# Loading and preparing the first row of the second part inside the attention's last pass

## The reference

```
x = x + attention(layernorm(x), Wq, Wk, Wv, Wo)        # 32 heads of 32, 8 key/value heads, rope, causal, softmax
x = x + autocorrelation(layernorm(x), ctx, ctx)        # spectra of q, k, v per channel; corr = ifft(qf * conj(kf)).real
                                                       # top 9 of the sums of corr, softmax, weighted shifted values
x = x + streams(layernorm(x), W_res, W_pre, W_post, ..., gate, W_branch)
        # 24 logits a token; a 4x4 matrix made doubly stochastic by 50 log-space iterations; y = (sum of streams) @ W_branch
```

## Time and profile before

| | us |
|---|---|
| median of 3 runs | 1199.89 |
| the profiled execution | 1201.8 |
| its span | 1200.0 |
| PE busy | 1027.2 |
| DVE busy | 907.2 |
| ACT busy | 600.5 |
| POOL busy | 447.7 |

### The profile page before, as it was taken

How to read it: one execution, slowest core, us unless ns; L and a number is a source line. 1 busy time by engine, 2 the same in 40 slices (tenths; PEclk the granted TensorE clock), 3 DMA queues, 4 the chain that set the end, 5 groups by cost and what they waited for, 6 DMA issues and landing times. The chain is left out here.

```text
span 1200.0 us, 23293 instructions
## 1 busy us (share of the span) xinstructions
PE 1027.2 (86%) x7874; PEld 761.2 (63%) x7874; DVE 907.2 (76%) x2830; ACT 600.5 (50%) x1787; POOL 447.7 (37%) x665
## 2 busy tenths in 40 slices
PE   5889999999999999999863899999999899833328
PEld 4667777877777777778643677777555565422215
DVE  6756886667876667866541787789999999899993
ACT  6624555445555445554433677776546555421215
POOL 0713433234433334333323466665334334203011
PEclk9989999999999999999967999999999999955759
DMA  9111011110111110111014214223222221119407
GB/s 378 39 43 51 28 60 59 59 42 22 54 59 59 50 50 18 59 60 43 25 36 151 79 53 132 93 75 113 95 75 92 76 75 54 48 29 333 130 6 188
DMA packets 47234, 95.71 MB, mean 80 GB/s; under 512 B 5952, under 2 KB 30400, under 8 KB 47168
## 3 DMA queue, kind: packets, MB, share of 16 engines
q1 hardware_dynamic: 47168, 94.91, 23.6%
HBM read 64.48 MB, written 27.26 MB: 76 GB/s over the span
## 5 line engine op out<-in xcount | busy, mean ns | idle before, releaser
L628 POOL TENSOR_TENSOR prob_G<-prob_G,rl 128x512 f32<-128x512 f32 x96 | 99.7, 1040 | 251.0 <-DVE rl L513 251.0
L390 ACT ACTIVATE prob_G<-prob_G,negm 128x128 f32<-128x128 f32 x384 | 149.4, 390 | 82.9 <-DVE negm L455 82.9
L245 PE MATMUL ps_qkv<-w_hi,xT_hi 128*128 128x512 f32 x384 | 156.1, 406 | 17.4 <-DVE prob_G L518 9.3
L246 PE MATMUL ps_qkv<-w_lo,xT_hi 128*128 128x512 f32 x384 | 151.0, 393 | 0.0
L247 PE MATMUL ps_qkv<-w_hi,xT_lo 128*128 128x512 f32 x384 | 150.7, 392 | 0.0
L319 PE MATMUL ps_qkv<-wo_hi,aT_hi 128*128 128x512 f32 x256 | 109.1, 426 | 0.0
L321 PE MATMUL ps_qkv<-wo_hi,aT_lo 128*128 128x512 f32 x256 | 103.1, 403 | 0.0
L320 PE MATMUL ps_qkv<-wo_lo,aT_hi 128*128 128x512 f32 x256 | 103.0, 402 | 0.0
L245 PEld LDWEIGHTS ps_qkv<-w_hi,xT_hi 128*128 128x128 f32 x384 | 72.6, 189 | 43.6 <-issue 20.6
L451 DVE TENSOR_TENSOR prob_G<-ps_s,mask 128x512 f32<-128x512 f32 x96 | 64.9, 676 | 43.9 <-PE ps_s L228 43.3
L480 DVE TENSOR_TENSOR xT_lo<-ps_t,xT_hi 128x512 fp32r<-128x512 f32 x16 | 11.1, 691 | 101.2 <-ACT xT_hi L418 101.2
(11 more groups left out here) (287 smaller groups left out, 2682.6 us busy)
## 6 DMA issues: line engine op xcount, KB each, us to landing
xin<-in_x SPq DMA_DIRECT2D x16, 512.0 KB, 3.3
xres<-in_x SPq DMA_DIRECT2D x16, 512.0 KB, 5.3
x<-xres SPq DMA_DIRECT2D x16, 512.0 KB, 2.6
c_xin<-x SPq DMA_DIRECT2D x16, 512.0 KB, 4.1
c_b_xres<-x SPq DMA_DIRECT2D x16, 512.0 KB, 3.3
rows_x<-c_row SPq DMA_DIRECT2D x64, 128.0 KB, 2.3
m_xm<-rows_x SPq DMA_DIRECT2D x16, 512.0 KB, 8.8
out<-m_ot SPq DMA_DIRECT2D x64, 128.0 KB, 2.3
```

Of the source, the lines that this page charges most:

```text
L245: nc.tensor.matmul(ps_qkv[:, n, :], xT_hi[:, k, :], w_hi[:, k, cols], start=k == 0, stop=False)
L246: nc.tensor.matmul(ps_qkv[:, n, :], xT_hi[:, k, :], w_lo[:, k, cols], start=False, stop=False)
L390: r = nc.scalar.activation(prob(g)[:, j, :], prob(g)[:, j, :], ACT.Exp, bias=negm[:, h:h + 1], accum_out=lsum[:, h:h + 1])
L628: nc.gpsimd.tensor_tensor(prob(g), prob(g), rl[:, g * GROUP:(g + 1) * GROUP].rearrange("p (j o) -> p j o", o=1).to_broadcast([P, GROUP, T] ...
```

## The change

Row 0's buffers of the second part and its constants no longer lie in tensors that are allocated with the second part. A new class `FirstRow` places them at addresses that the attention's projection weights `w_hi` and `w_lo` hold, and keeps them through the second and third part. In the attention's last pass, SP waits until the last projection has read these weights (`qkv_ps` at 3 * B) and issues the eight loads there, between the load of the last residual and the store of the last row. ACT, DVE and POOL do the split of the matrices and of row 0 and its normalisation at the end of what they have in that pass, DVE ahead of the residual. PE's order is the same. Eight tensors of the third part (`m_xm0` to `m_xm7`) are placed by the new class too, and nothing else of the third part changes.

```diff
+class FirstRow:
+    def __init__(self, nc, kept):
...
+        with ExitStack() as shared:
+            self.place(shared, "c_")
+        with ExitStack() as shared:
+            self.mixed = [shared.enter_context(nc.sbuf_tensor(f"m_xm{n}", [P, NS, C], F32)) for n in range(MIXED_IN_FIRST)]
...
                     sp.dma_start(xres[:], x[b]).then_inc(xres_in, 16)
+                    if not project:
+                        sp.wait_ge(qkv_ps, 3 * B)
+                        sp.dma_start(row0.xin[:], x1[0]).then_inc(row0.x_in, 16)
+                        sp.dma_start(row0.mats[:, 0:FWD_W, :], dft[:, 0:FWD_W, :]).then_inc(row0.fwd_in, 16)
+                        sp.dma_start(row0.cin[:], ctx_in[0]).then_inc(row0.cin_in, 16)
+                        sp.dma_start(row0.mats[:, FWD_W:N_DFT, :], dft[:, FWD_W:N_DFT, :]).then_inc(row0.const_in, 16)
+                        sp.dma_start(row0.idf[:], ident).then_inc(row0.const_in, 16)
+                        sp.dma_start(row0.w24_sb[:], w24).then_inc(row0.const_in, 16)
+                        sp.dma_start(row0.base_sb[:], base).then_inc(row0.const_in, 16)
+                        sp.dma_start(row0.wb_sb[:], wb.rearrange("(k p) n -> p k n", k=2)).then_inc(row0.const_in, 16)
...
                     attend_out(1)
+                    if not project:
+                        act.wait_ge(row0.fwd_in, 16)
+                        nc.scalar.activation(row0.fwd_hi[:, :, :], row0.mats[:, 0:4, :], ACT.Copy).then_inc(row0.fwd_hi_done, 1)
+                        act.wait_ge(row0.cin_in, 16)
+                        nc.scalar.activation(row0.c_hi0[:], row0.cin[:], ACT.Copy).then_inc(row0.chi_done, 1)
+                        act.wait_ge(row0.x_in, 16)
+                        act.wait_ge(x1_nb_done, 1)
+                        nc.scalar.activation(row0.xn[:], row0.xin[:], ACT.Identity, bias=norm2[:, 0, 1:2],
+                                             scale=norm2[:, 0, 0:1]).then_inc(row0.xn_done, 1)
+                        act.wait_ge(row0.xn_done, 1)
+                        nc.scalar.activation(row0.xn_hi[:], row0.xn[:], ACT.Copy).then_inc(row0.xnh_done, 1)
...
                     attend_out(1)
+                    if not project:
+                        dve.wait_ge(row0.fwd_hi_done, 1)
+                        nc.vector.tensor_tensor(row0.fwd_lo[:, :, :], row0.mats[:, 0:4, :], row0.fwd_hi[:, :, :].bitcast(F32),
+                                                ALU.subtract).then_inc(row0.fwd_lo_done, 1)
...
                     x1_scale(b - 1)
+                if not project and attend:
+                    pool.wait_ge(row0.chi_done, 1)
+                    TT(row0.c_lo0[:], row0.cin[:], row0.c_hi0[:].bitcast(F32), ALU.subtract).then_inc(row0.clo_done, 1)
+                    pool.wait_ge(row0.xnh_done, 1)
+                    TT(row0.xn_lo[:], row0.xn[:], row0.xn_hi[:].bitcast(F32), ALU.subtract).then_inc(row0.xnl_done, 1)
```

More of the change, by code:

```diff
@@ L44, with sem, place, sb @@
 AX = mybir.AxisListType
-def attention_phase(nc, x, wqkv, wo, ident, causal, rope, x1, norm2):
+MIXED_IN_FIRST = 8
+class FirstRow:
+    def __init__(self, nc, kept):
+        self.nc = nc
+        def sem(name):
+            return kept.enter_context(nc.semaphore("c_" + name))
+        self.const_in, self.fwd_in, self.x_in, self.cin_in = sem("const_in"), sem("fwd_in"), sem("x_in"), sem("cin_in")
+        self.fwd_hi_done, self.fwd_lo_done = sem("fwd_hi_done"), sem("fwd_lo_done")
+        self.xn_done, self.xnh_done, self.xnl_done = sem("xn_done"), sem("xnh_done"), sem("xnl_done")
+        self.chi_done, self.clo_done = sem("chi_done"), sem("clo_done")
+        with ExitStack() as shared:
+            self.place(shared, "c_")
+        with ExitStack() as shared:
+            self.mixed = [shared.enter_context(nc.sbuf_tensor(f"m_xm{n}", [P, NS, C], F32)) for n in range(MIXED_IN_FIRST)]
+    def place(self, stack, prefix):
+        def sb(name, shape, dt=F32, on=stack):
+            return on.enter_context(self.nc.sbuf_tensor(prefix + name, shape, dt))
+        with ExitStack() as shared:
+            whole = sb("c_whole0", [P, D], F32, shared)
+        lo = sb("c_lo0", [P, D], F32R)
+        tensors = (whole, lo, sb("c_hi0", [P, D], F32R), sb("b_idf", [P, P]), sb("mats", [P, N_DFT, P]), sb("fwd_hi", [P, 4, P], F32R),
+                   sb("fwd_lo", [P, 4, P], F32R), sb("w24_sb", [P, KD, NLOG]), sb("base_sb", [P, NLOG]), sb("wb_sb", [P, 2, C]),
+                   sb("xin", [P, D]), sb("xn", [P, D]), sb("xn_hi", [P, D], F32R), sb("xn_lo", [P, D], F32R), sb("cin", [P, D]))
+        if prefix == "c_":
+            (self.c_whole0, self.c_lo0, self.c_hi0, self.idf, self.mats, self.fwd_hi, self.fwd_lo, self.w24_sb, self.base_sb, self.wb_sb,
+             self.xin, self.xn, self.xn_hi, self.xn_lo, self.cin) = tensors
+def attention_phase(nc, x, wqkv, wo, ident, causal, rope, x1, norm2, row0, ctx_in, dft, w24, base, wb):
     with ExitStack() as ctx:
@@ L777, in weave, with autocorrelation_phase @@
             advance(dve, chain, to, 1)
-def autocorrelation_phase(nc, x1, ctx_in, ident, dft, w24, base, wb, norm2, facts, chains, rows_x, rows_y):
+def autocorrelation_phase(nc, x1, ctx_in, row0, norm2, facts, chains, rows_x, rows_y):
     with ExitStack() as ctx:
@@ L793, in sem @@
             return ctx.enter_context(nc.semaphore("c_" + name))
[L795 to L805, removed]
-        xres = sb("b_xres", [P, D])
[L807 to L814, removed]
+        idf, mats, fwd_hi, fwd_lo, w24_sb, base_sb, wb_sb = (row0.idf, row0.mats, row0.fwd_hi, row0.fwd_lo, row0.w24_sb,
+                                                             row0.base_sb, row0.wb_sb)
+        xin, xn, xn_hi, xn_lo, cin = row0.xin, row0.xn, row0.xn_hi, row0.xn_lo, row0.cin
+        xres = sb("b_xres", [P, D])
+        c_hi = [row0.c_hi0, sb("c_hi1", [P, D], F32R)]
+        with ExitStack() as shared:
+            c_whole = [row0.c_whole0, shared.enter_context(nc.sbuf_tensor("c_c_whole1", [P, D], F32))]
+        c_lo = [row0.c_lo0, sb("c_lo1", [P, D], F32R)]
         k_spec = [sb(f"k_spec{i}", [P, D]) for i in range(2)]
@@ L1215, in _ @@
         def _(act):
-            act.wait_ge(fwd_in, 16)
-            nc.scalar.activation(fwd_hi[:, :, :], mats[:, 0:4, :], ACT.Copy).then_inc(fwd_hi_done, 1)
             def split_context(n, par):
@@ L1395, in _ @@
         def _(dve):
-            dve.wait_ge(fwd_hi_done, 1)
-            nc.vector.tensor_tensor(fwd_lo[:, :, :], mats[:, 0:4, :], fwd_hi[:, :, :].bitcast(F32),
-                                    ALU.subtract).then_inc(fwd_lo_done, 1)
             def beside(b, part):
@@ L1677, in _, with mixing_phase @@
             iterations(pool, body)
-def mixing_phase(nc, rows_x, rows_y, facts, chains, gate, sel, fold, out):
+def mixing_phase(nc, row0, rows_x, rows_y, facts, chains, gate, sel, fold, out):
     with ExitStack() as ctx:
@@ L1694, in mixing_phase @@
         RING = 3
-        xm = [sb(f"xm{n}", [P, NS, C]) for n in range(B)]
+        xm = row0.mixed + [sb(f"xm{n}", [P, NS, C]) for n in range(MIXED_IN_FIRST, B)]
         ym = [sb(f"ym{n}", [P, C]) for n in range(B)]
@@ L1996, in build @@
         norm2 = kept.enter_context(nc.sbuf_tensor("norm2", [P, B, 2], F32))
-        attention_phase(nc, x, wqkv, wo, ident, causal, rope, x1, norm2)
+        row0 = FirstRow(nc, kept)
+        attention_phase(nc, x, wqkv, wo, ident, causal, rope, x1, norm2, row0, ctx, dft, w24, base, wb)
+        row0.place(kept, "kept_")
         facts = kept.enter_context(nc.sbuf_tensor("facts", [P, B, FACTS], F32))
@@ L2002, in build @@
             first_row += n
-        autocorrelation_phase(nc, x1, ctx, ident, dft, w24, base, wb, norm2, facts, chains, rows_x, rows_y)
-        mixing_phase(nc, rows_x, rows_y, facts, chains, gate, sel, fold, out)
+        autocorrelation_phase(nc, x1, ctx, row0, norm2, facts, chains, rows_x, rows_y)
+        mixing_phase(nc, row0, rows_x, rows_y, facts, chains, gate, sel, fold, out)
 def rope_tables():
```

22 lines of the change are left out of this document (5 added, 17 removed).

## The result

| | before | changed |
|---|---|---|
| median of the first comparison (4 runs each) | 1200.07 us (1199.0 to 1200.85) | 1189.53 us (1187.94 to 1192.48) |
| profiled execution, span | 1201.8, 1200.0 | 1188.75, 1186.9 |
| mean of all runs of this study | 1202.6 (51 runs) | 1189.0 (15 runs) |

The ratio of the first comparison is 0.9898, interval 0.9878 to 0.9917: faster, by 10.5 us on the medians. Two later comparisons of the same two kernels, on two different chips, gave 0.9905 (0.9885 to 0.9925) and 0.9865 (0.984 to 0.989). The kernel before was measured on a third chip as well, beside some of the experiments; the last line of the table pools all of this. The predicted 1186.9 was 2.6 us too low, inside its range of 1184.2 to 1190.2. (One run of the kernel before with 5,700 us, and one of an experiment with 1,388 us, are left out throughout.)

What follows compares the result with a forecast made beforehand. PE bounds the kernel but waits 17.2 us at the seam, 13.20 of it for row 0's preparation behind the barrier. 13.0 us gained, nothing added, clock 0: 1199.89 - 13.0 = 1186.9 us, range 1184.2 to 1190.2.

Steps and rivals of the forecast that it cites:

- The removed 13.20 us: Row 0's loads and preparation between the barrier (632.50) and 645.70, all said to leave that stretch.
- PE's 0.22 us: PE's response from last release to first matmul, said to stay behind the barrier, so PE starts at 632.72.
- The last pass hides it: Attention's last pass: loads and operations fit each queue's idle time, adding nothing; tightest cover is POOL's, 5.9 us.
- The clock: At the seam: after 4.25 us of idle time PE starts as cold as before, so zero gained or lost.
- the rival of the holding clock: At the seam: clock stays 1.00 or is lost for part of twelve matmuls; up to 2.4 us more, 1184.5; chance 0.16.
- The bound of 2.4: Most that row 0's twelve matmuls to the first key spectrum could gain at full clock, in us.
- The fall in the next gap: Rival: clock falls in the 2.5 us gap before the first transform back, costing 3.4 us, 1190.3; chance 0.08.
- PE's own start: Rival: PE coming straight through the barrier needs up to 3.5 us to start; gain 9.7 us, 1190.2; chance 0.08.
- The gain carries: Second part keeps the whole gain after row 0; rival: part is lost, 1193.4 if half; chance 0.05.
- the sign that the prediction named: In the second part: a smaller shift at row 5 than at row 0 would show the prediction wrong.
- The level: Whole kernel: 13.0 us subtracted from the median 1199.89 gives 1186.9; for the profiled execution, 1201.8 gives 1188.8.
- The likeliest case: Whole kernel: the forecast itself, a time within 0.9 us of 1186.9; chance 0.58.

Runs made afterwards that it cites:

- the loads alone: Changed kernel with only the eight loads kept in the attention's last pass, row 0's operations back behind the barrier; 1196.66 us median of 12, ratio 0.9955 to the kernel before.
- the constants alone: Changed kernel with row 0's x and context loaded, split and normalised behind the barrier, constants' six loads and matrices' split staying early; 1197.81 us median, ratio 0.9961.
- the two repeats: The changed kernel, unaltered, measured and profiled twice more; 1189.1 us median of 6 and 1188.48 us median of 5.
- PE filled at the seam: Changed kernel plus 16 matmuls that nobody reads behind the attention's last output chunk; 1186.76 us median of 5.
- its filled versions: Changed kernel plus 16 unread matmuls at the seam, without or with 8 more ahead of the transform back; 1186.76 and 1186.85 us medians.
- The version with 18 matmuls ahead of the barrier: Changed kernel with row 0's 18 matmuls moved ahead of the barrier behind the attention's last output chunk; 1184.31 us median of 5, repeated 1186.14.
- the two delayed versions: Changed kernel with the eight loads held back for ACT's last attention split, or for half the output projection; 1188.71 and 1199.82 us medians.

## Why the prediction was right

*The removed 13.20 us, and PE's 0.22 us.* Right: PE starts 0.22 us behind the barrier (632.56 - 632.34) and its gap is 4.32 us where 4.25 were forecast. The experiments with the loads alone and with the constants alone show what the 13.2 consisted of.

*The last pass hides it.* Right in each queue. The matrices landed later than forecast, ACT waited 1.59 us for them, and `fwd_hi` started at 616.52 and not 615.2; `xn_lo` ended at 623.70 where 623.36 was forecast, and the cover on POOL was 5.36 us where 5.9 was. It isn't the same each time: in the two repeats POOL idled 5.6 and 3.6 us there, the latter with a context that landed 8.0 us after its issue. Delaying the loads by 4.6 us cost nothing; delaying them by 15.4 us (610.50 to 625.88) cost 9.8 at the barrier, which is close to 15.4 less the cover of 5.4: beyond it the price is about one for one.

*The clock.* Taken as zero, as cold as before, and that holds only for the first profile, where the clock fell 1.9 us into the gap. In both repeats it held through the gap and fell 0.9 and 0.7 us after PE's start, which is what the rival of the holding clock described. Its gain was small even so: from PE's start to the first key spectrum 5.08 us in the first profile and 4.6 in the two repeats, against 5.39 before, so 0.3 to 0.8 us. The bound of 2.4 was nearly right too: with PE kept busy it is 2.0 to 2.3. The fall in the next gap did not occur in any of the changed kernel's three profiles. It did with PE filled at the seam. Its price was mis-sized: 1.6 us, not 3.4, as the clock rises again before the transform is over.

*PE's own start.* This rival falls. Wherever all of its inputs were ready, PE's first matmul came 0.22 or 0.23 us behind SP's first DMA, with nothing else to wait for (the changed kernel, its delayed and its filled versions). The rule cited from the Trainium skill (Runtime: NRT & Kernel Launch, the section Instruction fetch mechanics), on code to be loaded behind a taken branch, does not show at this barrier; the 0.22 us leave no room for it here. Whether the branch led outside of what had been fetched, no run shows.

*The gain carries.* Nearly. The second part took 431.69 us from its first key spectrum to its end before and 432.71 after, so 1.0 us was lost in it. By ACT's first copy of each row's correlation the shift is 13.5 us at row 0, 13.8 at row 5, 14.1 from row 8 to row 14, and 12.5 at row 15. So the sign that the prediction named, a smaller shift at row 5 than at row 0, stayed away; why the shift grew by 0.7 us was not looked into. One step, between rows 14 and 15, lost 1.7 us:

```profile
991.76 4.54 PE L1057 MATMUL pair<-c_c_whole,c_mats 128*128 128x512 f32 x6 [1.17 <-DVE c_x L1494]
```

And before:

```profile
1005.91 2.84 PE L1012 MATMUL pair<-c_c_whole,c_mats 128*128 128x512 f32 x6 [1.17 <-DVE c_x L1459]
```

Stretches of the changed kernel:

```profile
990.00:992.00 2.00, 0.83 (x3) 0.99 0.00 0
992.00:994.00 2.00, 2.00 (x3) 0.50 0.63 209
994.00:996.00 2.00, 2.00 (x4) 0.66 0.13 53
```

And of the kernel before, at the same place of its program:

```profile
1004.00:1006.00 2.00, 0.83 (x3) 1.00 0.00 0
1006.00:1008.00 2.00, 2.00 (x5) 1.00 0.43 147
```

The same gap of 1.17 us, the same matmuls; in one the clock falls behind it and in the other it doesn't. Of the 13 profiles of this study seven have the fall at this step and six don't; two others have one or two falls between 830 and 940 us. The version with 18 matmuls ahead of the barrier has it in one profile and not in the other, so the program alone doesn't decide it. But all three profiles of the changed kernel have it and the only one of the kernel before lacks it. That the change has no part in it is therefore not shown.

*The level.* This is the step that was off, by 1.9 of the 2.6 us. The gain was subtracted from the median of the three runs shown (1199.89). Over 51 runs the kernel before has a mean of 1202.6, so these three were on its fast side: of the 47 later runs, on three chips, 14 are at or below 1200.85, and all four of the first comparison are. Whether that was luck or its chip is open. The sum had been made against the profiled execution of 1201.8; 1201.8 - 13.0 = 1188.8 was written down beside it, and that is what the changed kernel does (1189.0 on the mean of 15). The gain itself was 13.0 forecast, 13.1 in the spans and 13.6 in the means of all runs, and 10.5 on the medians of the first comparison. That 13.0 came out so well is in part luck: the seam gave 13.5 with the clock, the rows behind it 0.7 more, one fall took 1.7, and the third part gave 0.7. The likeliest case's own 0.9 us either way was too narrow for a kernel whose runs spread over 4 to 9 us.

Open: why the kernel before spreads further (1198.1 to 1207.3) than the changed one (1186.4 to 1192.5). The granted clock goes with it, but the one profile of the kernel before is of an execution of 1201.8 us without a fall between 700 and 1010, so that where its longer runs lose the 5 us was not seen. How much of the 13.6 us in the means is the seam's can't be told from the times alone.

## What to carry to other kernels

At a barrier between two parts, look at what the next part's first matmul waits for: loads and preparation that need no result of the part before can move under its last pass, and the gain here was the whole chain from the barrier on, as each queue that they were put in had more idle time than they took. Watch the queue whose next work sets the barrier; here it was POOL, with 3.6 to 5.6 us to spare. Where the clock can fall, read a gain from a milestone well behind it and from several profiles: the matmuls that kept PE busy at the seam gave 2.0 us there and next to nothing by row 14. Subtract a gain from a level that many runs support, or from the execution it was worked out in, not from the median of three.

## What the runs showed of the hardware

A gap of PE as short as 1.2 us, in a stretch where it was busy 0.83 of 2.00 us, can be followed by the clock's fall from 2.4 to 1.2 GHz, and the same gap in another execution is not: seven profiles of 13 have the fall there. It costs 1.7 us each time (six matmuls in 4.54 us instead of 2.84); in the transform back a fall cost 1.6 us. At the seam the fall came 1.9 us after PE had stopped in the changed kernel's first profile and 5.3 us after it in the kernel before; in the two repeats it came 5.2 and 5.0 us after it, when PE had started again and had run three and two matmuls at full clock.

Loads of one kind landed later when issued while the residual's load was still under way: ACT could take the matrices 5.6, 5.0 and 5.8 us after their issue in the three profiles of the changed kernel, and 3.7 and 3.6 us after it in the two delayed versions, which issued them when that load was over; in the kernel before it was 4.05. PE's first matmul behind the barrier came 0.22 or 0.23 us after SP's first DMA in the seven profiles in which its inputs were ready; in the one where a matmul without waits stood first (633.10 against 633.13), it came 0.03 us ahead of it.
